# Moving the weighted values of the last stage one slot and taking out its filler products: a decoder block on one Trainium2 core

## Chip, cores and metric

The kernel runs on 1 core of one Trainium2 chip. The metric is device microseconds (us) of one execution, lower is better; the median of 3 runs before the change is 2255.5 us (2255.46 to 2257.71).

## What is computed

The input is `x`, 64 sequences of 64 tokens with 256 channels, and a context `ctx_512`, 64 sequences of 64 tokens with 64 channels. Three residual blocks follow each other:

```python
x = x + _L0_attn_ref(_layernorm(x), ...)            # gated delta rule, 16 heads, causal convolutions
x = x + _L0_xattn_ref(_layernorm(x), ctx, ctx)      # 32 query heads of 8 channels, 8 key/value heads
x = x + _L0_ffn_ref(_layernorm(x), w1, b1, w2, b2)  # 256 -> 1024 -> 256, ternary weights, exact gelu
```

The change touches the last two, which the kernel runs together as its last stage. There, for each token, 32 heads of softmax attention over 64 context tokens are added to `x`; the sum is normalised, multiplied by ternary `w1`, sent through gelu, multiplied by ternary `w2`, and added with `b2`.

## The kernel before

The rows are cut into G = 8 groups of 512 tokens (8 sequences). The first two stages (normalisation and gates, then the delta rule head by head) fill the first 1805 us. The last stage, lines 1050 to 1600 and their counterparts on the other engines, goes group by group, and each group in 8 **slots** (`u` = 0 to 7). All engines have the order of their work written out by hand as loops over group `i` and slot `u`; semaphores tie them together, and no scheduler moves anything. The last loops begin at lines 893 (ACT), 1206 (DVE), 1555 (PE) and 692 (POOL).

In the text below a slot's pieces have short names:

- **S**(u), `scores`, line 1476: scores of slot u on PE, 16 small products, issued two slots ahead: slot u of the PE loop issues S(u+2). It waits until DVE has subtracted the maxima (`sub_done`) of slot u, since the two pairs of PSUM banks alternate.
- `shifted_scores`, lines 1177 and 1181: DVE takes the maximum of one half of a slot's scores and subtracts it; two calls (j = 0, 1) in a slot.
- `exponentials`, line 872: ACT, two in a slot.
- **T**(u), `transposes_of`, line 1495: PE transposes the exponentials; `transposed`, line 879: ACT copies them out.
- **W**p, `weighted`, line 1509: PE weights the values of a quarter p (0 to 3) of the group, two slots' worth; it waits for the copies of those slots.
- `attended` (line 1189 on): DVE divides by the sums, adds to `x` and takes statistics, for the same quarter. After quarters 1 and 3 come `moments` (1151, 1154; DVE), `rstd_half` (674; POOL, a power of -0.5), and `normalized_half` (1162, 1167, 1169; DVE), all for that **half** of the group (256 tokens). `normalized_half` stands in the DVE order between the two `shifted_scores` of its slot.
- **HT**, `half_transposed`, line 1462: PE transposes the normalised half; `ffn_rows`, line 866: ACT copies it out.
- `hidden`, line 1523: PE's first feed-forward product of a half, in four blocks f of 8 products, and `gelus`, line 888: ACT. ACT loads its gelu table before them and its exponential table after. The blocks use the same PSUM banks as T, so T of the next slot waits for all four gelus (`gelu_done`).
- `two_parts`, lines 686 and 688: POOL splits each gelu block into two 16-bit parts.
- **Sm**, `summed`, line 1537: PE's second feed-forward product, each call four of eight blocks; `results`, line 1204: DVE adds the finished half; the sync engine's queue (SP) then stores a finished group (540) and loads rows of a later one (535), read by `arrived` (1133 on; DVE).
- RT, `rows_transposed`, line 1454, prepares the next group's queries.
- The **filler**, `keep_busy`, line 1547: products of the identity with zeros, accumulated into the bank of the second product (`F2B`). They change no value.

Group i's PE loop also does the feed-forward work of group i-1's second half and most of its first half, and W3 of group i-1.

Of the kernel before, what the change touches and what calls it, by code (L numbers as in the profile page):

```python
# [60 lines left out]
def build(nc, x, ctxT, ctxR, wall, wo, wab, cw, w1, b1, w2, b2, cst, out):  # L61
    ctx = ExitStack()
    with ctx:
# [146 lines left out]
        S = {n: sem(n) for n in names}  # L210
# [7 lines left out]
        def at(count):  # L218

            return count + 1  # L220
# [342 lines left out]
        def _(pool):  # L563
# [107 lines left out]
            def rstd_half(i, hf):  # L671
                cols = slice(2 * hf, 2 * hf + 2)
                pool.wait_ge(S["ln_b"], at(7 * (2 * i + hf) + 5))
                nc.gpsimd.tensor_tensor(RSTD[:, 1, cols], VE[:, 1, cols], MHALF[:, 0:2], ALU.pow).then_inc(S["rstd_b"], 1)  # L674
# [3 lines left out]
                xv = XC[i % 3][:, 2 * hf:2 * hf + 2, :]  # L678
                nc.gpsimd.tensor_tensor(xv, xv, B2[:, :][:, None, :].broadcast_to([P, 2, E]), ALU.add).then_inc(S["b2_done"], 1)

            def two_parts(i, hf):
                n = 2 * i + hf
                for f in range(4):
                    pool.wait_ge(S["gelu_done"], at(4 * n + f + 1))
                    pool.wait_ge(S["f2_mm"], at(max(n - 1, 0)))
                    nc.gpsimd.tensor_copy(HH[hf][:, f, :], H[hf][:, f, :]).then_inc(S["hh_done"], 1)
                    pool.wait_ge(S["hh_done"], at(4 * n + f + 1))
                    nc.gpsimd.tensor_tensor(HL[hf][:, f, :], H[hf][:, f, :], HH[hf][:, f, :], ALU.subtract).then_inc(S["hl_done"], 1)
# [3 lines left out]
            for i in range(G + 1):  # L692
                live, last, following = i < G, i > 0, i + 1 < G
                if last:
                    rstd_half(i - 1, 1)
                    two_parts(i - 1, 0)
                if following:
                    rstd_rows(i + 1)
                if last:
                    biased(i - 1, 1)  # L700
                if live:
                    rstd_half(i, 0)
                if last:
                    two_parts(i - 1, 1)
                if following:
                    value_blocks(i + 1)
                if live:
                    biased(i, 0)
# [3 lines left out]
        def _(act):  # L712
# [179 lines left out]
            for i in range(G + 1):  # L892
                live, last, following = i < G, i > 0, i + 1 < G
                for u in range(8):
                    if live:
                        exponentials(i, u)
                        transposed(i, u)
                    if u in (0, 4) and last:
                        gelus(i - 1, u // 4)
                    if u == 2 and last:  # L900
                        ffn_rows(i - 1, 1)
                    if u == 5 and following:
                        queries(i + 1)
                    if u == 6 and live:
                        ffn_rows(i, 0)


# [1 line left out]
        def _(dve):  # L909
# [298 lines left out]
            for i in range(G + 2):  # L1208
                live, last, following = i < G, 0 < i <= G, i + 1 < G
                for u in range(8):  # L1210
                    if live:
                        shifted_scores(i, u, 0)
                    if u == 2 and last:
                        normalized_half(i - 1, 1)
                    if u == 6 and live:
                        normalized_half(i, 0)
                    if live:
                        shifted_scores(i, u, 1)
                    if u == 0 and i >= 2:
                        results(i - 2, 1)  # L1220
                    if u == 1 and last:
                        attended(i - 1, 3)
                        moments(i - 1, 1)
                    if u in (3, 5, 7) and live:
                        attended(i, u // 2 - 1)
                    if u == 3 and following:
                        arrived(i + 1)
                    if u == 4 and last:
                        results(i - 1, 0)
                    if u == 4 and following:  # L1230
                        normalized(i + 1)
                    if u == 5 and live:
                        moments(i, 0)


# [1 line left out]
        def _(pe):  # L1237
# [242 lines left out]
            def transposes_of(i, u):  # L1480
                if u in (1, 5) and i:
                    pe.wait_ge(S["gelu_done"], at(4 * (2 * i - 2 + u // 4) + 4))
                if u == 6 and i + 1 < G:
                    pe.wait_ge(S["qt_done"], at(2 * i + 4))
                for j in range(2):
                    n = 16 * i + 2 * u + j
                    pe.wait_ge(S["exp_done"], at(n + 1))
                    if n >= 2:
                        pe.wait_ge(S["pt_done"], at(n - 1))
                    if j == 1 and u == 3 and i:  # L1490
                        pe.wait_ge(S["xh2"], at(2 * i))
                    if j == 1 and u == 7:
                        pe.wait_ge(S["xh2"], at(2 * i + 1))
                    for q in range(4):
                        ins = nc.tensor.transpose(TRB[j][:, P * q:P * q + P], ES[n % 8][:, P * q:P * q + P], ident)  # L1495
                    ins.then_inc(S["pt_mm"], 1)
# [58 lines left out]
            for i in range(G + 1):  # L1555
                live, last, following = i < G, i > 0, i + 1 < G
                for u in range(8):
                    fill = live and u not in (0, 4)
                    if fill and u in (1, 5) and i:
                        pe.wait_ge(S["x3_done"], at(2 * i - 2 + u // 4))  # L1560
                    if u < 6 and live:
                        scores(i, u + 2)
                    if u >= 6 and following:
                        scores(i + 1, u - 6)
                    if u == 0 and last:
                        weighted(i - 1, 3)
                    if u in (2, 4, 6) and live:
                        weighted(i, u // 2 - 1)
                    if fill:
                        keep_busy(12 if u in (1, 5) else 6)  # L1570
                    if live:
                        transposes_of(i, u)
                    if u in (0, 4) and last:
# [2 lines left out]
                        hidden(i - 1, u // 4)  # L1576
                    if u == 2 and last:
                        summed(i - 1, 0, range(0, 4))
                        if live:
                            pe.wait_ge(S["pt_done"], at(16 * i + 6))  # L1580
                        else:
                            pe.wait_ge(S["gelu_done"], at(8 * i - 4))
                        half_transposed(i - 1, 1)
                    if u == 3 and last:
                        summed(i - 1, 0, range(4, 8))
                    if u == 5 and following:
                        pe.wait_ge(S["pt_done"], at(16 * i + 12))
                        rows_transposed(i + 1)
                    if u == 6 and last:
                        summed(i - 1, 1, range(0, 4))  # L1590
                    if u == 6 and live:
                        pe.wait_ge(S["pt_done"], at(16 * i + 14))
                        half_transposed(i, 0)
                    if u == 7 and last:
                        summed(i - 1, 1, range(4, 8))


_NAMES = ["x", "ctxT", "ctxR", "wall", "wo", "wab", "cw", "w1", "b1", "w2", "b2", "cst"]
# [44 lines left out]
```

## Time and profile before

| | us |
|---|---|
| median of 3 runs | 2255.5 |
| the profiled execution | 2261.75 |
| its span, first to last instruction | 2260.0 |
| last stage, from its first products to the end | about 452 |

The times of the rows below are from the profiled execution. The mean granted TensorE clock over the span is 0.986 of full speed. Timeline rows give start, duration, engine, line, operation, and in brackets the idle time of that engine just before, with what ended it. Products overlap a little, so that the distance between two starts says more than a row's duration.

### The profile page before, as it was taken

To read this page: it belongs to the slowest core of one execution; us is meant where nothing else is said; L and a number is where in the kernel's file an instruction comes from. 1 tells how busy PE (TensorE), PEld (TensorE's weight loads), DVE (VectorE), ACT (ScalarE), POOL (GpSimd) and SP (SyncE) were. 2 spreads that over 40 slices of the span, in tenths; PEclk is the share of its full clock that TensorE was granted. 3 is DMA by queue.
4 is the path that set the end of the run, shared out by engine and by line. 5 is a ranking of instruction groups with operands and counts; after the bars stand their busy time and mean duration, and the time that the engine had idled before them with its cause. 6 is when DMAs were issued, how large, how long until landed. Compare 5 with 4: busy or idle time off the path is not lost.

```text
span 2260.0 us, 60686 instructions
## 1 busy us (share of the span) xinstructions
PE 2066.4 (91%) x23176; PEld 1320.7 (58%) x23176; DVE 1841.9 (81%) x2894; ACT 1538.5 (68%) x2881; POOL 1026.2 (45%) x1376
## 2 busy tenths in 40 slices
PE   2489799999999999999999999999988789999997
PEld 2234366566665666656666565665555467777776
DVE  6788788888888888898988989888866567777774
ACT  3489677777777777777777777777756535666654
POOL 1005765372835538273563827446290113334434
PEclk9999999999999999999999999999999989999999
DMA  8536423243232433323243342333322120111100
GB/s 285 191 119 203 149 77 101 81 102 98 74 99 75 107 82 95 101 71 103 81 100 85 89 104 75 96 88 84 91 67 60 31 61 12 35 53 36 37 21 20
DMA packets 360813, 199.91 MB, mean 88 GB/s; under 512 B 304336, under 2 KB 313296, under 8 KB 358608
## 3 DMA queue, kind: packets, MB, share of 16 engines
q1 hardware_dynamic: 360528, 196.04, 30.8%
q8 instruction: 188, 3.08, 0.6%
q14 instruction: 97, 0.79, 0.1%
HBM read 123.87 MB, written 72.09 MB: 87 GB/s over the span
## 4 chain that ended last, share of the span: by engine, by line
PE 71%; ACT 11%; issue 6%; DVE 4%; POOL 4%; DMA 2%; SPq 1%; ACTq 0%; POOLq 0%; DVEq 0%
PE PS L1297 22%; PE PS L1311 15%; PE PS L1375 6%; PE PS L1390 5%; ACT XN L790 4%; PE PS L1348 3%; ACT Y L767 3%; PE PS L1476 3%; PE PS L1509 3%; PE PS L1547 3%; PE PS L1495 2%; PE PS L1332 2%; PE PS L1537 2%; PE PS L1339 2%; DMA XP<-in_x 1%
## 5 line engine op out<-in xcount | busy, mean ns | idle before, releaser
L1036 DVE SCALAR_TENSOR_TENSOR Y<-PS,CW,Y 128x504 f32<-128x504 f32 (+2 forms) x1536 | 1114.1, 732 | 233.9 <-ACT Y L760 200.0
L1297 PE MATMUL PS<-XT,WH 128*128 128x512 f16 x2048 | 617.3, 383 | 6.3 <-DVE Y L1036 6.3
L760 ACT ACTIVATE Y<-PS,CW 128x512 f32<-128x512 f32 x512 | 394.4, 773 | 324.2 <-PE PS L1297 320.3
L1297 PE MATMUL PS<-XT,WL 128*128 128x512 f16 x1024 | 390.7, 382 | 0.0
L1311 PE MATMUL PS<-WOS,XN 128*128 128x256 f16 x3072 | 380.0, 274 | 2.7 <-DVE XN L1051 1.7
L1311 PEld LDWEIGHTS PS<-WOS,XN 128*128 128x128 f16 x3072 | 301.9, 98 | 95.0 <-issue 3.1
L586 POOL TENSOR_SCALAR KD<-SCR 128x32 f32<-128x32 f32 x16 | 5.8, 362 | 660.9 <-DMA SCR<-PGD 660.9
L611 POOL TENSOR_TENSOR SCR<-SCR 128x31 f32<-128x31 f32 (+15 forms) x496 | 284.9, 574 | 38.9
L1297 PEld LDWEIGHTS PS<-XT,WH 128*128 128x128 f16 x2048 | 168.9, 98 | 209.0 <-issue 42.2
L608 POOL TENSOR_TENSOR SCR<-SCR 128x31 f32<-128x31 f32 (+15 forms) x496 | 271.4, 547 | 38.9
L790 ACT ACTIVATE XN<-PS,KN 128x256 f32<-128x256 f32 x512 | 212.7, 466 | 16.4 <-PE PS L1311 16.4
L766 ACT ACTIVATE XN<-Y 128x512 f16<-128x512 f32 x256 | 160.0, 625 | 76.8 <-PE PS L1311 75.0
L1051 DVE TENSOR_TENSOR XN<-Y,XN 128x512 f16<-128x512 f32 x256 | 192.0, 750 | 10.0 <-ACT Y L767 10.0
L1375 PE MATMUL PS<-XN,M 64*64 64x256 f32 x2048 | 140.1, 387 | 45.5 <-ACT XN L790 45.2
L1297 PEld LDWEIGHTS PS<-XT,WL 128*128 128x128 f16 x1024 | 100.7, 98 | 122.5 <-issue 2.4
L773 ACT ACTIVATE KQ<-Y 128x512 f32<-128x512 f32 x256 | 159.6, 623 | 11.1 <-DVE W L1026 6.4
L767 ACT ACTIVATE Y<-Y 128x512 f32<-128x512 f32 x256 | 157.6, 615 | 0.0
L879 ACT ACTIVATE WH<-PS 128x512 f32<-128x512 f32 x128 | 70.6, 596 | 125.4 <-PE PS L1495 125.4
L1390 PE MATMUL PS<-KQ 128*64 128x128 f32 x2048 | 140.1, 279 | 4.6 <-ACT SCR L804 3.9
L1390 PEld LDWEIGHTS PS<-KQ 128*64 128x64 f32 x2048 | 109.2, 136 | 56.1 <-issue 49.4
L1375 PEld LDWEIGHTS PS<-XN,M 64*64 64x64 f32 x2048 | 77.0, 132 | 107.3 <-issue 98.8
L674 POOL TENSOR_TENSOR RSTD<-VE,MHALF 128x2 f32<-128x2 f32 x16 | 11.3, 707 | 202.5 <-DVE VE L1154 202.5
(140 smaller groups left out, 2976.7 us busy)
## 6 DMA issues: line engine op xcount, KB each, us to landing
PGD<-SCR SPq DMA_DIRECT2D x128, 256.0 KB, 2.1
SCR<-PGD SPq DMA_DIRECT2D x128, 256.0 KB, 3.2
EQD<-XN SPq DMA_DIRECT2D x32, 512.0 KB, 2.6
SCR<-EQD SPq DMA_DIRECT2D x128, 128.0 KB, 2.6
SCR<-QND SPq DMA_DIRECT2D x128, 128.0 KB, 3.1
SCR<-in_wall SPq DMA_DIRECT2D x8, 1024.0 KB, 7.2
SCR<-PGD SPq DMA_DIRECT2D x64, 128.0 KB, 3.2
ED<-SCR SPq DMA_DIRECT2D x16, 512.0 KB, 2.7
```

Of the source, the lines that this page charges most:

```text
L608: nc.gpsimd.tensor_tensor(t, LP[:, j, j + 1:BL][:, :, None].broadcast_to([P, n, m]), LY[:, j, 0:m][:, None, :].broadcast_to([P, n, m]), AL ...
L611: nc.gpsimd.tensor_tensor(LY[:, j + 1:BL, 0:m], LY[:, j + 1:BL, 0:m], t, ALU.subtract).then_inc(S["lane"], 1)
L760: A_.activation(Y[:, b, :], PJ[b][:, :], ACT.Identity, scale=CW[:, h[1] % NH, cw0 + 3:cw0 + 4], bias=CW[:, h[1] % NH, cw0 + 4:cw0 + 5]).th ...
L766: A_.activation(VHL[:, 0, b, :], Y[:, b, :], ACT.Silu)
L767: A_.activation(Y[:, b, :], Y[:, b, :], ACT.Silu).then_inc(S[f"silu{b}"], 1)
L790: ins = A_.activation(VW[:, a, :], VWB[:, E * i:E * i + E], ACT.Copy, scale=KN[:, kn, l:l + 1])
L1036: V_.scalar_tensor_tensor(yv[:, :, m:T], pv[:, :, 0:T - m], CW[:, h[1] % NH, cw0 + 3 - m:cw0 + 4 - m], yv[:, :, m:T], ALU.mult, ALU.add).t ...
L1051: V_.tensor_tensor(VHL[:, 1, b, :], Y[:, b, :], VHL[:, 0, b, :], ALU.subtract).then_inc(S["vl_done"], 1)
L1297: ins = mm(PJ[b][:, :], wt[:, c, w0:w0 + P], XT[:, g % 3, xi, :], start=(n == 0), stop=(n == 5))
L1311: ins = mm(VWB[:, E * i:E * i + E], VHL[:, vk, n, P * a:P * a + P], WOS[:, wk, 2 * (w[1] % NH) + n, :], start=(t == 0), stop=(t == 5))
L1375: ins = mm(AC[a % 2][r:r + 64, E * (a // 2):E * (a // 2) + E], M[b, off % 2, a, :], VW[b, a, :], start=(off % NH == 0 and a < 2), stop=(of ...
L1390: ins = mm(gram[64 * n:64 * n + 64, a], KQ[:, s, 0, c0:c0 + 64], KQ[:, s, :, c0:c0 + 64], start=True, stop=True)
```

## The change

On PE, W moves from slots 0 (W3 of the group before), 2, 4, 6 to slots 1, 3, 5, 7. HT moves from slots 2 and 6 to 3 and 7, and then stands behind the slot's Sm, where in slot 6 it stood behind the first four blocks. All `keep_busy` calls inside the groups go, with the wait on `x3_done` ahead of them; the 136 products ahead of the groups stay. DVE's `attended`, `moments`, `normalized_half` and `results` follow one slot later, ACT's `ffn_rows` too. On POOL `two_parts` is cut in two, with `rstd_half` between.

```diff
 # POOL
                 if last:
+                    two_parts(i - 1, 0, (0, 1))
                     rstd_half(i - 1, 1)
-                    two_parts(i - 1, 0)
+                    two_parts(i - 1, 0, (2, 3))
...
                 if last:
                     biased(i - 1, 1)
+                    two_parts(i - 1, 1, (0, 1))
                 if live:
                     rstd_half(i, 0)
                 if last:
-                    two_parts(i - 1, 1)
+                    two_parts(i - 1, 1, (2, 3))
 # ACT
-                    if u == 2 and last:
+                    if u == 3 and last:
                         ffn_rows(i - 1, 1)
-                    if u == 6 and live:
+                    if u == 7 and live:
                         ffn_rows(i, 0)
 # DVE
-                    if u == 2 and last:
+                    if u == 3 and last:
                         normalized_half(i - 1, 1)
-                    if u == 6 and live:
+                    if u == 7 and live:
                         normalized_half(i, 0)
                     if live:
                         shifted_scores(i, u, 1)
-                    if u == 0 and i >= 2:
+                    if u == 0 and last:
+                        attended(i - 1, 2)
+                    if u == 1 and i >= 2:
                         results(i - 2, 1)
-                    if u == 1 and last:
+                    if u == 2 and last:
                         attended(i - 1, 3)
                         moments(i - 1, 1)
-                    if u in (3, 5, 7) and live:
-                        attended(i, u // 2 - 1)
+                    if u in (4, 6) and live:
+                        attended(i, u // 2 - 2)
...
-                    if u == 4 and last:
+                    if u == 5 and last:
                         results(i - 1, 0)
-                    if u == 5 and live:
+                    if u == 6 and live:
                         moments(i, 0)
 # PE, in transposes_of
-                    if j == 1 and u == 3 and i:
+                    if j == 1 and u == 4 and i:
                         pe.wait_ge(S["xh2"], at(2 * i))
-                    if j == 1 and u == 7:
-                        pe.wait_ge(S["xh2"], at(2 * i + 1))
+                    if j == 1 and u == 0 and i:
+                        pe.wait_ge(S["xh2"], at(2 * i - 1))
 # PE, the loop
-                    fill = live and u not in (0, 4)
-                    if fill and u in (1, 5) and i:
-                        pe.wait_ge(S["x3_done"], at(2 * i - 2 + u // 4))
...
-                    if u == 0 and last:
+                    if u == 1 and last:
                         weighted(i - 1, 3)
-                    if u in (2, 4, 6) and live:
+                    if u in (3, 5, 7) and live:
                         weighted(i, u // 2 - 1)
-                    if fill:
-                        keep_busy(12 if u in (1, 5) else 6)
...
                     if u == 2 and last:
                         summed(i - 1, 0, range(0, 4))
+                    if u == 3 and last:
+                        summed(i - 1, 0, range(4, 8))
                         if live:
-                            pe.wait_ge(S["pt_done"], at(16 * i + 6))
+                            pe.wait_ge(S["pt_done"], at(16 * i + 8))
                         else:
                             pe.wait_ge(S["gelu_done"], at(8 * i - 4))
                         half_transposed(i - 1, 1)
-                    if u == 3 and last:
-                        summed(i - 1, 0, range(4, 8))
...
-                    if u == 6 and live:
-                        pe.wait_ge(S["pt_done"], at(16 * i + 14))
-                        half_transposed(i, 0)
                     if u == 7 and last:
                         summed(i - 1, 1, range(4, 8))
+                    if u == 7 and live:
+                        pe.wait_ge(S["pt_done"], at(16 * i + 16))
+                        half_transposed(i, 0)
```

PE in slots 0 to 2 of a middle group. Before, from S(2) on; line 1509 is W (first W3 of the group before, then W0 of this), 1495 is T, 1523 `hidden`, 1547 the filler, 1537 Sm:

```order
L1476 MATMUL PS<-WL,KQ 64x256 x8
L1509 MATMUL PS<-VB,WH 64x18 x32
L1495 MATMUL PS<-CST,WL 128x128 x8
L1523 MATMUL PS<-XB,W 128x256 x32
L1476 MATMUL PS<-WL,KQ 64x256 x8
L1547 MATMUL PS<-SQ,IDH 128x256 x12
L1495 MATMUL PS<-CST,WL 128x128 x8
L1476 MATMUL PS<-WL,KQ 64x256 x8
L1509 MATMUL PS<-SCR,WH 64x18 x32
L1547 MATMUL PS<-SQ,IDH 128x256 x6
L1495 MATMUL PS<-CST,WL 128x128 x8
L1537 MATMUL PS<-W,WH 128x256 x16
```

W3 stood ahead of T(0) and `hidden`, so that `hidden` came between it and the next S. Now, from S(2) to T(3), with lines four higher (1480 S, 1499 T, 1527 `hidden`, 1513 W, 1541 Sm):

```order
L1480 MATMUL PS<-WL,KQ 64x256 x8
L1499 MATMUL PS<-CST,WL 128x128 x8
L1527 MATMUL PS<-XB,W 128x256 x32
L1480 MATMUL PS<-WL,KQ 64x256 x8
L1513 MATMUL PS<-VB,WH 64x18 x32
L1499 MATMUL PS<-CST,WL 128x128 x8
L1480 MATMUL PS<-WL,KQ 64x256 x8
L1499 MATMUL PS<-CST,WL 128x128 x8
L1541 MATMUL PS<-W,WH 128x256 x16
L1480 MATMUL PS<-WL,KQ 64x256 x8
L1513 MATMUL PS<-SCR,WH 64x18 x32
L1499 MATMUL PS<-CST,WL 128x128 x8
```

W3 now stands where the filler stood, behind `hidden` and S(3). Between W3 and S(5), the third S after `hidden`, PE has T(1), S(4), T(2) and one Sm.

POOL over one group, now (674 is `rstd_half`, 686 and 688 a block of `two_parts`, 669 and 679 other work):

```order
L686 CAST WH<-WOS 128x512
L688 TENSOR_TENSOR WH<-WOS,WH 128x512
L686 CAST WH<-WOS 128x512
L688 TENSOR_TENSOR WH<-WOS,WH 128x512
L674 TENSOR_TENSOR RSTD<-VE,MHALF 128x2
L686 CAST WH<-WOS 128x512
L688 TENSOR_TENSOR WH<-WOS,WH 128x512
L686 CAST WH<-WOS 128x512
L688 TENSOR_TENSOR WH<-WOS,WH 128x512
L669 TENSOR_TENSOR RSTD<-VE,MHALF 128x4
L679 TENSOR_TENSOR WOS<-WOS,B 128x512
```

`rstd_half` stood ahead of all four blocks and now stands between the second and the third.

## Rows read from the trace of the kernel before

**Rows 1.** The page, busy time of each engine over the whole span.
```profile
PE 2066.4 (91%) x23176; PEld 1320.7 (58%) x23176; DVE 1841.9 (81%) x2894; ACT 1538.5 (68%) x2881; POOL 1026.2 (45%) x1376
```

**Rows 2.** Busy time in one middle group, and its filler among the groups by line.
```profile
1990.00:2041.16 51.16, 46.79 (x650) 37.02 (x652) 39.31 (x78) 32.06 (x57) 21.18 (x24) 1.00 0.14 38
...
L1547 PE MATMUL PS<-SQ,IDH 128*128 128x256 f16 x48 | 6.3, 274 | 0.0
```

**Rows 3.** Timeline of PE: Sm, HT, T(7), then slots 0 and 1 of the next group.
```profile
2020.34 1.91 PE L1537 MATMUL PS<-W,WH 128*128 128x256 f16 x16
2022.09 0.61 PE L1462 MATMUL PS<-IDH,XB 128*128 128x128 f16 x8
...
2024.33 1.18 PE L1495 MATMUL PS<-CST,WL 128*128 128x128 f32 x8
...
2027.18 1.09 PE L1476 MATMUL PS<-SCR,KQ 32*64 32x256 f32 x16
2028.21 2.05 PE L1509 MATMUL PS<-SCR,WH 128*64 128x18 f32 x64
2030.18 1.09 PE L1495 MATMUL PS<-CST,WL 128*128 128x128 f32 x8
...
2036.02 1.09 PE L1476 MATMUL PS<-SCR,KQ 32*64 32x256 f32 x16
...
2039.01 1.13 PE L1495 MATMUL PS<-CST,WL 128*128 128x128 f32 x8 [0.48 <-issue]
```

**Rows 4.** Timeline of ACT, behind the last gelu of the same stretch.
```profile
2036.98 1.28 ACT L872 ACT_TABLE_LOAD   x1
2038.28 1.15 ACT L872 ACTIVATE WL<-WL 128x512 f32<-128x512 f32 x2
```

**Rows 5.** Timeline of DVE: `attended` to the next slot's last subtraction, two cases.
```profile
2004.94 0.35 DVE L1189 RECIPROCAL U0S<-PS 128x32 f32<-128x32 f32 x1
...
2012.91 0.69 DVE L1181 TENSOR_TENSOR WL<-PS,MX 128x512 f32<-128x512 f32 x1
...
2030.55 0.35 DVE L1189 RECIPROCAL U0S<-PS 128x32 f32<-128x32 f32 x1
...
2034.00 1.02 DVE L1162 TENSOR_SCALAR XN<-WOS,MV,RSTD 128x256 f32<-128x256 f32 x2
...
2038.04 0.69 DVE L1181 TENSOR_TENSOR WL<-PS,MX 128x512 f32<-128x512 f32 x1
```

**Rows 6.** Timeline of PE in the first group, where S waited for DVE.
```profile
1827.46 1.09 PE L1476 MATMUL PS<-SCR,KQ 32*64 32x256 f32 x16 [2.79 <-DVE WL L1181]
...
1845.53 1.98 PE L1476 MATMUL PS<-SCR,KQ 32*64 32x256 f32 x16 [2.12 <-DVE WL L1181]
1847.44 3.61 PE L1509 MATMUL PS<-VB,WH 128*64 128x18 f32 x64
1850.98 1.97 PE L1495 MATMUL PS<-CST,WL 128*128 128x128 f32 x8
```

**Rows 7.** Stretches: PE, PEld, DVE, ACT, POOL busy, then granted clock, DMA share, GB/s.
```profile
1655.00:1660.00 5.00, 3.45 (x32) 1.49 (x27) 3.36 (x5) 2.83 (x6) 4.53 (x7) 0.78 0.52 118
1705.00:1710.00 5.00, 3.45 (x47) 2.21 (x45) 3.68 (x6) 3.67 (x7) 0.00 (x0) 1.00 0.12 41
1850.00:1855.00 5.00, 5.00 (x46) 3.44 (x45) 3.70 (x11) 2.23 (x4) 1.54 (x3) 0.50 0.00 0
```

**Rows 8.** Timelines: T(1) of groups 1 and 7, the last T(7), POOL's last block.
```profile
1885.51 1.13 PE L1495 MATMUL PS<-CST,WL 128*128 128x128 f32 x8 [0.48 <-issue]
...
2195.63 1.13 PE L1495 MATMUL PS<-CST,WL 128*128 128x128 f32 x8 [0.48 <-issue]
...
2229.22 1.17 PE L1495 MATMUL PS<-CST,WL 128*128 128x128 f32 x8 [0.98 <-ACT WL L872]
...
2253.89 1.15 POOL L688 TENSOR_TENSOR WH<-WOS,WH 128x512 f16<-128x512 f32 x1
```

**Rows 9.** Timeline of SP's queue: the load of a later group's rows.
```profile
2030.80 0.34 SPq L535 DMA_DIRECT2D WOS<-X1D  x1
```

More of the change, by code:

```diff
@@ L679, in biased, with two_parts @@
                 nc.gpsimd.tensor_tensor(xv, xv, B2[:, :][:, None, :].broadcast_to([P, 2, E]), ALU.add).then_inc(S["b2_done"], 1)
-            def two_parts(i, hf):
+            def two_parts(i, hf, fs):
                 n = 2 * i + hf
-                for f in range(4):
+                for f in fs:
                     pool.wait_ge(S["gelu_done"], at(4 * n + f + 1))
@@ L1218, in _ @@
                         shifted_scores(i, u, 1)
-                    if u == 0 and i >= 2:
+                    if u == 0 and last:
+                        attended(i - 1, 2)
+                    if u == 1 and i >= 2:
                         results(i - 2, 1)
-                    if u == 1 and last:
+                    if u == 2 and last:
                         attended(i - 1, 3)
                         moments(i - 1, 1)
-                    if u in (3, 5, 7) and live:
-                        attended(i, u // 2 - 1)
+                    if u in (4, 6) and live:
+                        attended(i, u // 2 - 2)
                     if u == 3 and following:
                         arrived(i + 1)
-                    if u == 4 and last:
-                        results(i - 1, 0)
                     if u == 4 and following:
                         normalized(i + 1)
-                    if u == 5 and live:
+                    if u == 5 and last:
+                        results(i - 1, 0)
+                    if u == 6 and live:
                         moments(i, 0)
```

## The prediction, made before the changed kernel ran

> **What bounds the kernel now.** I read the page first: over the whole span PE is busy 91%, DVE 81%, ACT 68% [rows 1]. The change lies in the last stage alone, so I took one middle group there. From 1990.00 to 2041.16 PE is busy 46.79 us of 51.16 at full clock, DVE 39.31, ACT 32.06 [rows 2]. PE is nearly full, but 6.3 us of it are 48 products of the filler [rows 2]. The useful PE work is therefore about 40.5 us, close to DVE's 39.3: with the filler gone, neither engine alone explains a period of 51, and what counts is who waits for whom.
>
> Next the timeline of PE [rows 3]. T(0) starts at 2030.18 and T(1) at 2039.01, 8.83 us later. Between them stand `hidden` and the gelus, which PE, ACT and PE again take in turn. T(1) comes when ACT has loaded its exponential table (2036.98, 1.28 us) and finished the first of two exponentials that start at 2038.28 [rows 4]. PE waits only 0.48 us there, because the filler lies in that stretch.
>
> Then the timeline of DVE [rows 5]. From `attended` to the subtraction that ends the slot of `normalized_half` it takes 2030.55 to 2038.04 + 0.69 = 8.18 us; in the other half 2004.94 to 2012.91 + 0.69 = 8.66. In the kernel before, W3 (2028.21) stands ahead of `hidden`, so this DVE chain runs beside the 8.83 us, and the S that needs its end comes after T(1). It costs nothing there. That is the cover to watch.
>
> **The change part by part.**
>
> *W behind `hidden`.* S(3) starts at 2036.02, 5.84 us after T(0), and takes 1.03 (2027.18 to 2028.21); W takes 1.97 to the next start and 2.05 to its end [rows 3]. W3 in slot 1 then ends 5.84 + 1.03 + 2.05 = 8.92 us after T(0). T(1) can't start before 8.83. So W3 fits exactly into the place of the 12 filler products, and this move alone gives back its 1.97 us and the 0.48 us of waiting.
>
> *What follows, one slot later.* The DVE chain now begins only when W3 ends, with nothing of `hidden` left beside it. S(5) needs the subtraction at its end, since S(u+2) waits for slot u and `normalized_half` now stands in slot 3 between the two subtractions. From W3's end: 0.07 us to start, as I take it, 8.18 (or 8.66) for the chain, 0.06 to release PE. PE has T(1), S(4), T(2) and one Sm for that time, 1.0 + 1.03 + 1.0 + 1.75 = 4.8 us (T is 1.09 long, less the overlap of 0.1; Sm 2020.34 to 2022.09) [rows 3]. T(2) waits for its exponential about 0.4 of it. **PE then stands idle for about 3.2 us in one piece**, waiting for DVE.
>
> *The rest of the half.* After S(5) PE does S 1.03, W0 1.97, T(3) 1.0, Sm 1.75, then HT; ACT copies it out and computes an exponential before T(4): 2022.09 to 2024.33 is 2.24 us [rows 3]. HT now stands behind Sm, right before the T that needs ACT, so these 2.24 us are on the path; in the kernel before S and filler covered them. Half a group, T(0) to T(4), is 8.92 + 0.07 + 8.18 + 0.06 + 1.03 + 1.97 + 1.0 + 1.75 + 2.24 = 25.2 us, or 25.7 with the slower chain. The other half is alike: RT fills part of the wait there, but its DVE chain ends last too. The period is **50.4 to 51.4, I take 50.9 us**, against 51.16 now. All of the 6.3 us of filler is lost to the wait.
>
> *The clock.* This is the larger part. In the first group S waited 2.79 us and 2.12 us for DVE [rows 6], and after the second wait the granted clock was 0.50, the 1.2 GHz level [rows 7]. S took 1847.44 - 1845.53 = 1.91 us, W 3.54, T about 1.9 [rows 6], in place of 1.03, 1.97 and 1.0. The new wait of 3.2 us is longer than both, and the same three follow it: S(5), W0, T(3). They cost 0.88 + 1.57 + 0.9 = 3.35 us more, and all are on the path. Then comes an Sm, 1.75 us at full clock, that doubles at 1.2 GHz; I count a third of it, 0.6. **A fall costs 4.0 us a group.** Bounds: 0 if the clock holds; 1.7 if it is back in the middle of W; 5.1 with all of Sm. I take 4.0 since the sequence S, W, T stands in the rows wholly at the low level, and nothing with the filler's shape comes before Sm.
> Idle of 1.55 in 5 us was followed by a low stretch once and not the other time (clock 0.78 against 1.00) [rows 7]; 3.2 is longer than any wait in these rows.
> The Trainium skill (TensorE: Matmul & The Clock Gate, section "HAM oscillation — how this bites in real kernels") sees the harm in idle gaps above a length that it gives, and this gap stays below it. By that rule the clock would hold and the time be the first rival's, 2257. The waits of 2.12 and 2.79 us [rows 6] speak against it.
>
> *First group.* It has no `hidden` and no Sm, and now no filler. After the wait of 2.79 us, which stays, I take its clock to be low throughout: 8 S at 1.91, 8 T at 1.9, 3 W at 3.54 and RT at 2 make 43.1 us, with some 2.5 of waits around RT and HT. HT to T(0) is 2.24 + 0.5, then 8.83 + 2 for a `hidden` half at the low level: 59.2 from 1827.46 to T(1) of group 1. Before it is 1885.51 - 1827.46 = 58.05 [rows 6, 8]. **About +1**, from -10 (full clock, DVE as the bound) to +5.
>
> *Between.* From T(1) of group 1 to T(1) of group 7 it is 310.12 us now [rows 8], a low stretch in group 6 included. Six periods of 50.9 are 305.4: **-4.7**, and with six falls +24.
>
> *End.* T(7) of the last group waits for its own exponential behind the DVE chain: T(1) to T(7) is about 34.5 (the rest of the half after T(0), 25.45 - 8.83 = 16.6, then 8.92 + 0.07 + 8.18 + 0.7) against 33.6 now [rows 8], **+0.9**. From the last T(7) to the end of the span it is 30.8 now. The first half's HT now comes behind Sm, and `hidden` waits for it; W3 comes behind that `hidden`; and the second HT waits for all of Sm, whose last blocks POOL makes after `rstd_half`. POOL's last four blocks, which set the end, begin about 3.4 us later: **+3.4** (2 to 5). One more fall in group 7: **+4.0**.
>
> *At no cost.* The wait on `x3_done` protected the filler's bank only. POOL is busy 21.18 of 51.16 [rows 2]; `rstd_half` behind two blocks of `two_parts` is covered, since these finish while PE is still in `hidden`, S(3) and W3, and DVE's `moments` come later. If POOL were late, `normalized_half` would be later by as much. The later `results` moves SP's store and load by about 3 us: the load issues at 2030.80 [rows 9] and `arrived` reads it some 14 us later, in the new order too. ACT's `ffn_rows` is counted in the 2.24.
>
> Sum: +1 - 4.7 + 24 + 0.9 + 3.4 + 4.0 = **+28.6 us**. Against the profiled execution that is 2261.75 + 28.6 = 2290.4; the median of the runs lies 6.25 us below that execution, so I predict **2284 us**.
>
> **The rivals.**
>
> *The clock holds over the 3.2 us.* Then +1 - 4.7 + 0.9 + 3.4 = +0.6, **2256 to 2257 us**, no change. For it: waits of 1.55 us do pass [rows 7]. Against it: rows 6. Chance 0.13.
>
> *Faster: the clock holds in the first group also.* Its filler cost there was paid at the low level, and without it DVE is the bound: -10 instead of +1, and with the shorter chain (50.4) another -3. That is 2255.5 + 0.6 - 11 - 3 = **2242 us**. It decides when the granted clock stays at 1.00 behind 1850. Against it: its 2.79 us wait is untouched. Chance 0.08.
>
> *Faster: PE stays the bound.* If the DVE chain ended by the time PE has done its Sm, the 3.2 us of waiting would go from one half and about 0.9 from the other, 4.1 of seven periods: 2256.5 - 29 = **2228 us**. That needs a chain of 5 us instead of 8.2, or a later consumer; DVE's order shows neither. Chance 0.05.
>
> **How the numbers follow.** About 0.2%, 4.5 us, is what a measurement here can tell from no change. Slower: the forecast, 0.74. Within 0.2%: the first rival, 0.13. Faster: the two others, 0.13. The forecast's own range is 2268 (1.7 us a fall) to 2302 (5.1 a fall, the slow chain, +5 in the first group). The range reaches down to the first rival: 2250 to 2302, which leaves out the faster rivals and little else.
>
> **What would show it.** In the profile after: PE idle of about 3 us in each group before S (line 1480) in slot 3, released by DVE's subtraction (line 1183); granted clock 0.5 behind it, W of 3.5 us there; no line 1551 inside groups; W3 directly behind S(3), and T(1) about 8.8 us after T(0). With the gap but the clock at 1.00, the first rival holds. A period under 48 us, or S waiting for nothing in slot 3, would make the central step wrong.

## The result, and the profile after

The changed kernel takes **2294.4 us** (median of 4 runs, 2285.44 to 2297.98) against 2256.4 us before on the same chip; the ratio is 1.0155 (95% interval 1.0133 to 1.0176). It is slower by 38 us. The forecast was 2284 us with a range of 2250 to 2302, and a chance of 0.74 for slower.

The profiled execution after took 2297.98 us with a span of 2296.2 us, at the upper end of its runs; the span before is 2260.0 us. The 36.2 us between the spans lie here:

| stretch | before | after | difference | forecast |
|---|---|---|---|---|
| start of the span to the last stage, S(2) of group 0 | 1827.46 | 1829.01 | +1.6 | 0 |
| S(2) of group 0 to T(1) of group 1 | 58.05 | 54.20 | -3.9 | +1 |
| T(1) of group 1 to T(1) of group 7 | 310.12 | 336.46 | +26.3 | +19.3 |
| T(1) of group 7 to the end | 64.4 | 76.5 | +12.2 | +8.3 |

The first row of the table isn't the change's: no instruction ahead of that place differs.

The page, busy time of each engine and the granted clock in 40 slices, answering [rows 1]. PE's busy time falls by only 6.6 us although 384 products are gone, since products at the low clock take longer, and the clock's digits are below 9 in the last stage:

```profile
PE 2059.8 (90%) x22792; PEld 1309.9 (57%) x22792; DVE 1851.9 (81%) x2894; ACT 1540.9 (67%) x2881; POOL 1021.7 (44%) x1376
...
PEclk9999999999999999999999999999999978888989
```

A stretch as long as one middle group after (56.08 us from T(1) to T(1)), by the view of stretches (PE, PEld, DVE, ACT, POOL busy, granted clock, DMA share, GB/s), answering [rows 2]. A group took 51.16 us before. The mean clock is 0.91 in place of 1.00. DVE works as long as before (38.6 us against 39.3), so it has not become the bound by its load:

```profile
1985.00:2041.08 56.08, 46.46 (x604) 36.19 (x602) 38.62 (x75) 32.38 (x56) 20.85 (x23) 0.91 0.12 34
```

The timeline of PE over one group after, from S(3) of the first half through the second, answering [rows 3]:

```profile
1993.50 1.09 PE L1480 MATMUL PS<-WL,KQ 32*64 32x256 f32 x16
1994.53 2.05 PE L1513 MATMUL PS<-VB,WH 128*64 128x18 f32 x64
...
2005.34 1.98 PE L1480 MATMUL PS<-WL,KQ 32*64 32x256 f32 x16 [3.57 <-DVE WL L1183]
2007.26 3.61 PE L1513 MATMUL PS<-SCR,WH 128*64 128x18 f32 x64
2010.79 1.97 PE L1499 MATMUL PS<-CST,WL 128*128 128x128 f32 x8
...
2017.95 1.18 PE L1499 MATMUL PS<-CST,WL 128*128 128x128 f32 x8 [0.61 <-ACT WL L874]
...
2026.82 1.12 PE L1499 MATMUL PS<-CST,WL 128*128 128x128 f32 x8
...
2035.67 1.09 PE L1480 MATMUL PS<-SCR,KQ 32*64 32x256 f32 x16 [1.28 <-DVE WL L1183]
...
2043.59 1.17 PE L1499 MATMUL PS<-CST,WL 128*128 128x128 f32 x8 [0.61 <-ACT WL L874]
```

W3 (1994.53) stands directly behind S(3), as planned. After T(1), S(4), T(2) and an Sm, S(5) waits 3.57 us for DVE's subtraction, and S, W and T behind it run at the low clock, and Sm, which then takes 3.31 us, in part: W takes 3.61 us where it takes 2.05 in the other half. The second half, T(4) at 2017.95 to T(0) at 2043.59, has no such wait and no fall, and takes 25.64 us. A first half, in groups 2 to 7, takes 28.8 to 30.3 us.

The waits of PE from 1890 to 2230 us, groups 1 to 6 and the first wait of group 7 (total us, times, longest). DVE's subtraction is now its largest wait; between the groups of the kernel before no product waited for it:

```profile
PE PS L1480 <- DVE WL L1183: 37.4, 19, 3.6
```

The timeline of DVE behind W3, answering [rows 5]: `attended`, `moments`, a first subtraction, `normalized_half` (1164, 1169, 1171), the second subtraction, and `arrived`, which finds its rows there and waits for nothing:

```profile
1996.62 0.36 DVE L1191 RECIPROCAL U0S<-PS 128x32 f32<-128x32 f32 x1 [6.78 <-PE PS L1513]
...
2000.09 1.57 DVE L1164 TENSOR_SCALAR XN<-WOS,MV,RSTD 128x256 f32<-128x256 f32 x2
...
2002.44 1.52 DVE L1171 TENSOR_TENSOR XB<-XN,XB 128x512 f16<-128x512 f32 x1
2003.88 0.68 DVE L1179 TENSOR_REDUCE MX<-PS 128x8 f32<-128x512 f32 x1
2004.60 0.69 DVE L1183 TENSOR_TENSOR WL<-PS,MX 128x512 f32<-128x512 f32 x1
2005.20 1.40 DVE L1135 BATCH_NORM_STATS2 STT<-WOS 128x6 f32<-128x256 f32 x4
```

From 1996.62 to 2004.60 + 0.69 it is 8.67 us, all of it behind W3. DVE has idled 6.78 us just before, so the work that makes PE late is not too much work but work that begins late.

### The profile page after: what moved, and what is told of

Same layout as the page of the kernel before. It is cut to its first block, busy times and chain, and to the rows that moved or that the text cites. A ratio compares the mean times of both kernels' runs of the same rounds, so it can differ in the third digit from the quotient of the medians.

```text
span 2296.2 us, 59904 instructions
## 1 busy us (share of the span) xinstructions
PE 2059.8 (90%) x22792; PEld 1309.9 (57%) x22792; DVE 1851.9 (81%) x2894; ACT 1540.9 (67%) x2881; POOL 1021.7 (44%) x1376
## 3 DMA queue, kind: packets, MB, share of 16 engines
q1 hardware_dynamic: 360528, 196.04, 30.3%
## 4 chain that ended last, share of the span: by engine, by line
PE 66%; ACT 11%; DVE 9%; issue 8%; POOL 3%; DMA 2%; SPq 1%; ACTq 0%; POOLq 0%; DVEq 0%
PE PS L1301 22%; PE PS L1315 15%; PE PS L1379 6%; PE PS L1394 5%; ACT XN L792 4%; PE PS L1352 3%; ACT Y L769 3%; PE PS L1513 3%; PE PS L1336 2%; PE PS L1480 2%; PE PS L1499 2%; PE PS L1343 2%; PE PS L1541 2%; DVE Y L1038 2%; PE PS L1527 1%
## 5 line engine op out<-in xcount | busy, mean ns | idle before, releaser
L1053 DVE TENSOR_TENSOR XN<-Y,XN 128x512 f16<-128x512 f32 x256 | 199.0, 777 | 10.8 <-ACT Y L769 10.8
L686 POOL CAST WH<-WOS 128x512 f16<-128x512 f32 x64 | 40.0, 624 | 189.3 <-ACT WOS L890 189.3
```

Source lines behind the costliest of these rows:

```text
L1053: V_.tensor_tensor(VHL[:, 1, b, :], Y[:, b, :], VHL[:, 0, b, :], ALU.subtract).then_inc(S["vl_done"], 1)
```

## The experiments

The filler products in the runs below add zeros and change no value. Medians of "before" beside them were 2256.7 to 2259.1 us.

### Each part alone: the filler taken out, the order left

```diff
 # PE, the loop of the kernel before
-                    fill = live and u not in (0, 4)
-                    if fill and u in (1, 5) and i:
-                        pe.wait_ge(S["x3_done"], at(2 * i - 2 + u // 4))
...
-                    if fill:
-                        keep_busy(12 if u in (1, 5) else 6)
```

> The kernel before with the filler inside the groups taken out and nothing moved. If the removed PE time came back whole (48 products, 6.3 us in each of 7 groups and more in the first): 2212 or less. If the clock held: T(1) and T(5) wait 2.0 us for the gelus where 12 products stood, and the 6s give back 0.67 each, a period of about 49.8, 2244. Theory (a wait of 2 us in one piece lets the clock fall, as 2.12 us did): two falls a group of about 3 us each, a period near 55, 2270 to 2295.

Measured: 2287.3 us (2283.03 to 2295.82), ratio 1.0144 (1.0114 to 1.0173). The timeline of PE, T(1), then T(5) and what follows it:

```profile
1993.42 1.13 PE L1495 MATMUL PS<-CST,WL 128*128 128x128 f32 x8 [1.90 <-issue]
...
2017.08 1.13 PE L1495 MATMUL PS<-CST,WL 128*128 128x128 f32 x8 [1.89 <-issue]
...
2021.13 1.98 PE L1476 MATMUL PS<-SCR,KQ 32*64 32x256 f32 x16 [0.73 <-issue]
2023.05 3.61 PE L1509 MATMUL PS<-SCR,WH 128*64 128x18 f32 x64
```

Without the filler PE waits 1.90 us ahead of T(1) and T(5), where it waited 0.48 [rows 3], and in most groups the clock is at its low level behind one of these two waits. The filler had not been idle ballast: taking it out costs 30 us by itself.

### The moves alone, with the old amounts of filler

```diff
 # PE, the loop of the changed kernel
+                    fill = live and u not in (0, 4)
+                    if fill and u in (1, 5) and i:
+                        pe.wait_ge(S["x3_done"], at(2 * i - 2 + u // 4))
...
+                    if fill:
+                        keep_busy(12 if u in (1, 5) else 6)
```

> The changed kernel with the filler of the kernel before put back in its amounts (12 in slots 1 and 5, 6 in 2, 3, 6, 7, with the wait on x3_done), so that the move alone is left. Theory: S(5) starts no earlier, since DVE's chain begins at W3's end; 12 products and 6 shorten PE's wait to about 1.5 us, below what let the clock fall each time, and 0.67 behind W0 and W2 is added to the path: a period of 52 to 53 with few falls, the first group again as in the kernel before, median 2265 (2258 to 2278). Rival (the move is harmless and all of the loss comes from taking the filler out): 2256, no change.

Measured: 2280.6 us (2279.31 to 2290.52), ratio 1.0111 (1.0084 to 1.0138). The timeline of PE at slot 3:

```profile
1999.49 1.82 PE L1480 MATMUL PS<-WL,KQ 32*64 32x256 f32 x16 [2.08 <-DVE WL L1183]
2001.24 3.61 PE L1513 MATMUL PS<-SCR,WH 128*64 128x18 f32 x64
```

The expectation of 2258 to 2278 us failed. The fillers ahead of the wait take some of it, but 2.08 us of 3.57 stay where about 1.5 was expected, and the clock falls behind them too, in every first half from group 1 to 7 of the profiled run, which is the slowest of the four. So the moves alone cost 23 us, and both parts together 38, not 53. That the two overlap because both pay for the same waits and falls is argued here, not shown.

### The long wait filled

```diff
                 for u in range(8):
+                    if u == 3 and live and last:
+                        keep_busy(26)
```

> The changed kernel with 26 products with zeros put into slot 3 of groups 1 to 7, ahead of S(5), where the profile shows the wait of 3.6 us for DVE (12 of them take 1.48 us, so 26 take about 3.0). They end before S(5) may start, so they change the granted clock and nothing else. Theory (the fall of the clock at that wait costs 4.1 us in each of 7 groups): S(5), W0, T(3) at 1.03, 1.97, 1.0 us, no low stretch behind slot 3, period 56.1 to about 51.5, median 2294 less 28, 2266 (2260 to 2272). Rival (the later DVE chain costs the time by itself and the clock is incidental): 2286 to 2298, as without them.

Measured: 2283.3 us (2268.86 to 2287.21, 6 runs), ratio 1.010 (1.007 to 1.013). The profiled run is the fastest. The timeline of PE, a first half and the beginning of the second:

```profile
1881.73 3.00 PE L1551 MATMUL PS<-SQ,IDH 128*128 128x256 f16 x26
1885.46 1.09 PE L1480 MATMUL PS<-WL,KQ 32*64 32x256 f32 x16 [0.73 <-DVE WL L1183]
1886.48 2.05 PE L1513 MATMUL PS<-SCR,WH 128*64 128x18 f32 x64
...
1905.96 1.56 PE L1480 MATMUL PS<-SCR,KQ 32*64 32x256 f32 x16 [0.79 <-DVE WL L1183]
```

With the place filled, S and W behind it are at full clock (W 2.05 us), and so they are in all six first halves. But the clock now falls once in each of the six second halves, behind waits of 0.7 to 1.3 us that had been there before. The six runs lie in two clumps, two near 2270 and four from 2281 to 2287, and the median is above the 2260 to 2272 of the theory. The profiled run, in spite of its falls in the second halves, lies inside that range; the slower runs have no profile, so what they lose stays open.

### Every wait filled

The same with 26 products in slot 3, 9 in slot 7, 5 on either side of RT.

```diff
                 for u in range(8):
+                    if live and last:
+                        keep_busy({3: 26, 6: 5 if following else 0, 7: 9}.get(u, 0))
...
+                        if last:
+                            pe.wait_ge(S["x3_done"], at(2 * i - 1))
+                            keep_busy(5)
                         rows_transposed(i + 1)
```

> The changed kernel with products with zeros in each long wait of groups 1 to 7: 26 ahead of S(5) in slot 3, 9 ahead of S(1) of the next group in slot 7 (wait 1.28 us), 5 ahead of RT and 5 ahead of the S behind it (waits 0.71 and 0.79). None lies on the path. Theory (with the waits filled the clock holds everywhere, and what is left of the loss is DVE's chain): halves of 25.64 us each, period 51.3, no low stretch in groups 1 to 7, profiled execution 2260 to 2266 and a median of 2262, with the wide spread of the run with 26 alone (2269 to 2287) gone. Rival (that spread has another cause, a slower DVE or ACT for example): 2275 to 2290 again.

Measured: 2284.6 us (2280.25 to 2287.74), ratio 1.0114 (1.0088 to 1.0139): the expectation failed. The timeline of PE, a second half:

```profile
1919.19 1.09 PE L1480 MATMUL PS<-SCR,KQ 32*64 32x256 f32 x16 [0.29 <-DVE WL L1183]
1920.21 2.05 PE L1513 MATMUL PS<-SCR,WH 128*64 128x18 f32 x64
1922.20 1.97 PE L1499 MATMUL PS<-CST,WL 128*128 128x128 f32 x8
```

PE waits 0.29 us here, and still the clock falls at T. It does so in every half, which takes 27.3 us in place of 25.64. The theory that idle time alone lets the clock fall is refuted. The theory formed from this: what stands ahead of each fall is S and W in a row, small products (32 rows, or 18 columns), while in the kernel before wide filler products followed W directly in slots 2 and 6. The contrast is not a clean one: in slots 0 and 4 of the kernel before T stood between W and the wide products of `hidden`, as here it stands between W and the equally wide ones of Sm.

### Wide products behind W

```diff
 # added to the kernel with every wait filled, ahead of T
+                    if live and last and u in (3, 7):
+                        keep_busy(6)
```

> e5_fill_waits with 6 wide filler products behind W in slots 3 and 7 of groups 1 to 7, ahead of T there. In e5 the clock fell once in every half, at T behind S and W, though PE had idled only 0.2 to 0.8 us before S; each half took 27.3 us where a half without a fall takes 25.64. Theory (narrow products alone bring the fall: S and W in a row, 64 of W's products having 18 columns; wide products behind W end it): the falls in the halves go, each half costs its 6 fillers, 0.67 us, more and loses the fall, 1.65 us less, so a period of about 52.6 us in place of 54.6 and, over six groups, 12 us less than e5: 2272 us (2266 to 2278). Rival (something else brings the fall, the idle time ahead of S or the mean load of PE): the falls stay at T or behind it, each half is 0.67 us longer, 2284 + 9 = 2293 us (2288 to 2298).

Measured: 2278.1 us (2276.3 to 2284.96), ratio 1.0101 (1.0079 to 1.0123). Stretches of 300 us, of the kernel with every wait filled and then of this one:

```profile
1900.00:2200.00 300.00, 274.24 (x3552) 216.78 (x3544) 220.15 (x421) 179.17 (x309) 115.16 (x127) 0.94 0.11 32
```

```profile
1890.00:2190.00 300.00, 274.37 (x3662) 218.54 (x3661) 222.65 (x430) 178.56 (x310) 117.37 (x129) 0.97 0.11 33
```

PE is busy 274 of 300 us in both, but since a product at the low clock is busy for longer, that is 3662 products against 3552; the clock is 0.97 in place of 0.94. Between T(1) of group 1 and that of group 7 the clock's record has 5 low stretches in place of 12, and a half without one takes 26.25 us, the 0.6 more that six fillers cost. The rival, 2293 us, is out. The theory's 12 us over six groups aren't reached either: between the two T(1) it is 324.67 us in place of 327.42, 2.8 us less, and 2.9 us of the difference of the profiles lie ahead of S(2) of group 0, where no instruction differs. That six more products behind W leave fewer falls is shown. Whether it is by their width or because a half then holds more work is not separated, and it is not the whole cause, since some halves still fall. What decides in those stays open, as does why first halves with the same pieces kept the clock when only the long wait was filled, and lost it here and there with more filler about.

### POOL's blocks ahead of the reciprocal root

```diff
 # POOL
-                    two_parts(i - 1, 0, (0, 1))
+                    two_parts(i - 1, 0, (0, 1, 2, 3))
                     rstd_half(i - 1, 1)
-                    two_parts(i - 1, 0, (2, 3))
```

and the same for the other half.

> The changed kernel with all four blocks of two_parts ahead of rstd_half on POOL, none behind it. POOL then has nothing to do beside normalized_half. Theory (DVE's normalized_half is 3.8 us long because POOL works beside it): it shrinks to about 2.5, the chain from W3's end to S(5) from 8.6 to 7.3, the wait ahead of S(5) from 3.57 to 2.3, the period by 2.6 with falls of the clock as before: median 2270 to 2282. Rival (POOL has no part in it): the chain stays 8.6, median 2285 to 2298; or rstd_half comes later behind four blocks and the time is longer.

Measured: 2273.2 us (2265.99 to 2278.08, 9 runs), ratio 1.006 (1.0044 to 1.0077), inside the theory's range. DVE's timeline over `normalized_half` (here 1161, 1166, 1168), then PE's at slot 3 (S is line 1477), in a first half:

```profile
1996.95 0.72 DVE L1161 TENSOR_SCALAR XN<-WOS,MV,RSTD 128x256 f32<-128x256 f32 x2
...
1998.18 0.69 DVE L1168 TENSOR_TENSOR XB<-XN,XB 128x512 f16<-128x512 f32 x1
1998.79 0.68 DVE L1176 TENSOR_REDUCE MX<-PS 128x8 f32<-128x512 f32 x1
```

```profile
2000.25 1.10 PE L1477 MATMUL PS<-WL,KQ 32*64 32x256 f32 x16 [1.73 <-DVE WL L1180]
```

With POOL idle beside it, `normalized_half` takes 1.84 us from start to the next start (1996.95 to 1998.79) in place of 3.79 (2000.09 to 2003.88 after), and the wait of PE is 1.73 us in place of 3.57. In the second halves of this run POOL's other work lies beside it, and it takes 3.16 us (2023.86 to 2027.02). In the changed kernel POOL's last two blocks run just then:

```profile
1998.92 0.71 POOL L674 TENSOR_TENSOR RSTD<-VE,MHALF 128x2 f32<-128x2 f32 x1 [3.63 <-DVE VE L1156]
...
2000.28 1.23 POOL L688 TENSOR_TENSOR WH<-WOS,WH 128x512 f16<-128x512 f32 x1
...
2002.21 1.21 POOL L688 TENSOR_TENSOR WH<-WOS,WH 128x512 f16<-128x512 f32 x1
```

The Trainium skill (SBUF — State Buffer, section "Who interferes with whom") says that a DVE instruction with two SBUF inputs contends with a GpSimd instruction that reads SBUF. The trace agrees: the subtraction with two SBUF inputs (1171) takes 1.52 us beside POOL and 0.69 without.

So moving two POOL blocks is worth 21 us. It does not undo something that the change brought in: in the kernel before POOL's blocks ran beside `normalized_half` too, and it took 3.80 us (2008.40 to 2012.20) in the slower of the two cases of [rows 5]:

```profile
2008.40 1.57 DVE L1162 TENSOR_SCALAR XN<-WOS,MV,RSTD 128x256 f32<-128x256 f32 x2
...
2010.75 1.52 DVE L1169 TENSOR_TENSOR XB<-XN,XB 128x512 f16<-128x512 f32 x1
2012.20 0.68 DVE L1177 TENSOR_REDUCE MX<-PS 128x8 f32<-128x512 f32 x1
```

```profile
2010.52 1.21 POOL L688 TENSOR_TENSOR WH<-WOS,WH 128x512 f16<-128x512 f32 x1
```

Nor is all of the 21 us the shorter chain. The theory left the falls as they were; the profile has six between T(1) of group 1 and that of group 7 in place of eight, three of them in first halves. Of 26.9 us saved there about 14 are the shorter halves (23.79 and 25.11 us without a fall, in place of 25.64 each), the rest falls; the first group took 5 us more.

### `normalized_half` behind the second subtraction

```diff
 # DVE
+                    if live:
+                        shifted_scores(i, u, 1)
                     if u == 3 and last:
                         normalized_half(i - 1, 1)
                     if u == 7 and live:
                         normalized_half(i, 0)
-                    if live:
-                        shifted_scores(i, u, 1)
```

> The changed kernel with normalized_half behind the second shifted_scores of its slot instead of between the two. Theory (S(5) waits because normalized_half, 3.4 to 3.8 us, stands ahead of the subtraction it needs): that subtraction ends 3.8 us earlier, about when PE has done its Sm; the wait of 3.6 us goes, with it the fall of the clock, and in the other half the 1.3 us; the halves become 22.0 and 24.3 us, the period 46 to 47, median about 2230 (2222 to 2240). Rival (something else is late next, HT waiting for the normalised half, or the clock falls in other waits): 2255 or more.

Measured: 2228.5 us (2223.98 to 2234.75), ratio 0.9872 (0.9848 to 0.9897): faster than before by 1.3%. The timeline of PE: T(1), S(5), and T(1) of the next group:

```profile
1931.84 1.12 PE L1499 MATMUL PS<-CST,WL 128*128 128x128 f32 x8
...
1937.04 1.09 PE L1480 MATMUL PS<-SCR,KQ 32*64 32x256 f32 x16
...
1978.73 1.12 PE L1499 MATMUL PS<-CST,WL 128*128 128x128 f32 x8
```

S(5) stands directly behind Sm, nothing in this period falls, and it is 46.89 us (1931.84 to 1978.73). `normalized_half` itself still takes 3.07 us (1936.79 to 1939.86), with a POOL block beside it; only its place differs. One swap in DVE's order turns the change from a loss of 38 us into a gain of 29. It also shows that no engine is too full for a period of 47 us; the place of `normalized_half` set the 56, by the wait and by the falls behind it. The same swap in the kernel before was not run, so how much of the gain needs the moves is not shown.

### Filler in the first group alone

Added to the kernel with `normalized_half` behind:

```diff
             scores(0, 1)
+            keep_busy(22)
...
                 for u in range(8):
+                    if i == 0:
+                        keep_busy({0: 0, 5: 26}.get(u, 4))
```

> The changed kernel with normalized_half behind the second subtraction, and products with zeros in the first group alone, where its PE waits for DVE: 22 ahead of the loop, 4 ahead of each S, 26 ahead of S(7). The run without them had 58 us of low clock in the first group and 60.4 us from S(2) to T(1) of group 1. Theory (without wide products nothing brings the clock back in the first group): full clock there, 43 to 48 us, median 2213 (2208 to 2220) against 2228. Rival (the first group is bound by DVE, or the added products cost what they bring): 2224 or more.

Measured: 2215.6 us (2211.93 to 2221.44), ratio 0.9812 (0.9783 to 0.984). From S(2) of group 0 to T(1) of group 1 it is 43.2 us (1820.50 to 1863.73) in place of 60.4 (1822.94 to 1883.38) without the filler. In the latter every S up to `hidden` took 1.98 us where it takes 1.09 at full clock.

### A faster version

Added to that: HT between the two halves of Sm's second call, so that ACT copies while PE multiplies, and `arrived` and the normalisation of the next group one slot later.

```diff
 # PE
-                        summed(i - 1, 0, range(4, 8))
+                        summed(i - 1, 0, range(4, 6))
...
                         half_transposed(i - 1, 1)
+                        summed(i - 1, 0, range(6, 8))
 # DVE
-                    if u == 3 and following:
+                    if u == 4 and following:
                         arrived(i + 1)
-                    if u == 4 and following:
+                    if u == 5 and following:
                         normalized(i + 1)
```

> The run with the first group's products and two more edits: HT between the two halves of its slot's Sm, so that Sm covers ACT's copy, and arrived and normalized one slot later on DVE, so that slot 4's subtraction does not wait behind arrived (S(6) waited 1.25 us for it). Theory: 1.2 us less in the first half and 0.6 in the second, seven groups: 11 to 13 us below the run without these edits, about 2201. Rival (PE's own work of 41 us a group and the 8.83 us between T(0) and T(1) already set the period): no change against that run.

Measured: **2204.6 us** (2203.45 to 2205.68), ratio 0.9759 (0.9734 to 0.9784). The timeline of PE from T(0) over T(4) to T(0): the wait ahead of T for the copied HT is gone, and the period is 44.94 us.

```profile
1995.19 1.09 PE L1499 MATMUL PS<-CST,WL 128*128 128x128 f32 x8
...
2016.51 1.09 PE L1499 MATMUL PS<-CST,WL 128*128 128x128 f32 x8
...
2040.13 1.09 PE L1499 MATMUL PS<-CST,WL 128*128 128x128 f32 x8
```

## Why the prediction was right

**The central step held.** "PE then stands idle for about 3.2 us in one piece, waiting for DVE" stands in the trace as 3.57 us ahead of S (line 1480) in slot 3, released by DVE's line 1183, in every middle group. W3 stands directly behind S(3), and T(1) comes 8.87 us after T(0) (2017.95 to 2026.82; 8.92 in the sum). The low clock and W of 3.6 us behind the wait are there as told. Filling the wait takes them away there, and so does moving its cause, without any filler; so the reason for the falls in the first halves is shown, not only the size. Filling alone gave back only 11 of the 38 us in the median, since the clock then fell in the second halves.

**A fall costs 4.0 us a group: measured 4.1.** First halves with a fall take 29.77 us on average, second halves without one 25.64, and first halves with the wait filled 25.62. The rival in which the clock holds falls with it. By the rule of the Trainium skill that the prediction weighed (TensorE: Matmul & The Clock Gate, section "HAM oscillation — how this bites in real kernels"), idle gaps shorter than its length should do no harm. The waits of 1.90 us without the filler, 2.08 us with the moves alone and 1.73 us with POOL's blocks ahead are all shorter than the one forecast, and the clock fell behind many of them: the measurements decide against it here. The wait of 3.57 us itself speaks neither way, since it came out longer than forecast, and longer than the length that the page gives.

**The period without falls was mis-sized a little, 50.9 against 51.3.** The sum took the DVE chain as 8.18 us in one half and 8.66 in the other [rows 5]; it took 8.67 and 8.68. "`rstd_half` behind two blocks of `two_parts` is covered" held for POOL's result, which is in time. What was mis-sized is the chain: in the kernel before POOL's blocks ran beside `normalized_half` in both cases, from before its start in that of 8.66 and from 0.18 us behind it in that of 8.18; in the new order two blocks begin ahead of it in both halves. The bound of 8.66 had held this case; its cause had not been seen, and the place of two POOL blocks turned out to be worth 21 us.

**"Six falls" should have been eight between the groups.** Two second halves fell too, 1.65 us each (27.3 us in place of 25.64), behind waits of 0.8 and 1.3 us; the prediction had seen that DVE's chain ends last there too, but counted no fall behind it. With 6 x 51.28 = 307.7 us, six falls of 4.14 and two of 1.65 it is 335.8, against 336.46 measured.

**The first group: +1 was forecast, -3.9 came.** "I take its clock to be low throughout" failed: it was full up to S(7) of that group and then low for 30.7 us, from the wait of 3.46 us on. The timeline of PE in the first group after, answering [rows 6]:

```profile
1829.01 1.09 PE L1480 MATMUL PS<-SCR,KQ 32*64 32x256 f32 x16 [2.79 <-DVE WL L1183]
...
1847.10 1.09 PE L1480 MATMUL PS<-SCR,KQ 32*64 32x256 f32 x16 [3.46 <-DVE WL L1183]
1848.12 3.61 PE L1513 MATMUL PS<-VB,WH 128*64 128x18 f32 x64
```

The wait of 2.79 us ahead of S(2) is the same in both kernels. Here the clock held behind it; in the kernel before it was low from 1828.5 on. With `normalized_half` behind, where the first group has the same products up to its last slots, it fell at once, and the group took 60.4 us, close to the 59.2 of the sum. So this term varied between profiles of kernels that are alike up to there, and no forecast of it from one profile could be firm; either value is inside the bounds, -10 to +5.

**The end: +8.3 was forecast, +12.2 came.** The path was right: POOL's last four blocks set the end (the last starts at 2290.12, was 2253.89 [rows 8]), and the second HT waits for Sm and that for POOL. One fall was counted in group 7; there were three. The timeline of PE in the drain:

```profile
2259.77 3.62 PE L1541 MATMUL PS<-W,WH 128*128 128x256 f16 x16
2263.18 1.06 PE L1466 MATMUL PS<-IDH,XB 128*128 128x128 f16 x8
...
2276.32 1.05 PE L1541 MATMUL PS<-W,WH 128*128 128x256 f16 x8 [3.06 <-POOL WH L688]
2278.23 1.89 PE L1541 MATMUL PS<-W,WH 128*128 128x256 f16 x8 [0.86 <-POOL WH L688]
```

Sm at 3.62 and 1.89 us (1.91 and 1.05 at full clock) and two HT at 1.06 (0.61) cost 3.5 us on the path, most of this term's error of 3.9 (the second HT, at 2279.91, is not among the rows).

**In sum** the forecast of +28.6 us for the profiled execution became +36.2, and the median of 2284 came out as 2294.4: the mechanism was right, the falls in places other than slot 3 were counted too low and the DVE chain a little, and the first group's -3.9 covers 5 us of that by luck. The profiled execution lay 3.6 us above its median, not 6.25, which is the rest. The upper end of the range, 2302, is some 3 us more than its own terms give (2284 + 7.7 for the falls, 3.5 for the slow chain, 4 for the first group); 2294.4 lies below either. The third rival, with PE as the bound, named its condition rightly, "a chain of 5 us instead of 8.2, or a later consumer": with `normalized_half` behind the subtraction the chain that S waits for takes 4.9 us (1931.96 to 1936.18 + 0.69), and the time is 2228.5 us.

## What to carry to other kernels

Before a filler goes, or work moves into its place, find what the wait beneath it ends on; here a chain of 8.7 us on an engine busy for 38.6 of 56 us set it, and one swap in that engine's order was worth 66 us of the changed kernel's time. Put ahead of a result that another engine waits for only what that result needs. Give a short wait on TensorE two prices, its length and the products behind it at the low clock; here 3.6 us of waiting cost 4.1 us more.

## What was not expected of the hardware

- The clock fell with TensorE almost full: with waits of at most 0.8 us in one piece it fell once in every half, behind scores and weighted values in a row (1.09 and 2.05 us). Six wide products more behind them in each half brought the falls between the groups from 12 to 5.
- A low clock stayed low with PE at work: in the first group of the version with `normalized_half` behind, PE waited at most 0.73 us at a time behind S(2) (1822.94), and every S, W and T took its longer time up to `hidden` (1873.94), whose 32 products took 6.51 us, the last of them at full clock.
- `normalized_half` on VectorE took 1.84 us alone and 3.79 us beside GpSimd's blocks; those blocks' subtractions took 1.21 to 1.23 us, where one with VectorE idle took 1.16 (1992.35).
